# Layer 0 of a graph network: which message tiles are kept whole in fp32 for the segment sum

## The reference, cut to what matters

```python
src, dst = (edge_index[0], edge_index[1])
msg = jax.nn.relu(x[src] + edge_attr @ W_e + b_e)          # (21250, 512)
aggr = jax.ops.segment_sum(msg, dst, num_segments=x.shape[0])
h = (1.0 + eps) * x + aggr
h = jax.nn.silu(_bn(h @ W1 + b1, g1, beta1))
h = h @ W2 + b2
return jax.nn.silu(_bn(h, g2, beta2))
```

## Time and profile before

| | us |
|---|---|
| median of 3 runs | 855.38 |
| the three runs | 850.87 to 858.94 |
| the profiled execution, its own time | 855.74 |
| its span, first to last instruction | 853.9 |
| mean granted TensorE clock | 0.971 of full |

### The profile page before, as it was taken

One profiled execution on the slowest core, in us unless ns is written; L12 is line 12 of the kernel. 1 busy time (PEld: TensorE's weight loads), 2 busy tenths in 40 slices (PEclk: granted clock), 3 DMA queues, 4 the chain that ended last, 5 costly groups with the idle time before them and its releaser, 6 DMA issues.

```text
span 853.9 us, 11369 instructions
## 1 busy us (share of the span) xinstructions
PE 781.4 (92%) x3714; PEld 629.9 (74%) x3714; DVE 638.5 (75%) x1120; ACT 448.8 (53%) x805; POOL 359.6 (42%) x381
## 2 busy tenths in 40 slices
PE   7899998888879999798699999999999999999993
PEld 5665655565569999686477878788867898989893
DVE  7889998898679826387598999999984253535365
ACT  4888988888554403211377777787761211111122
POOL 6777777777300000023777777777700000000011
PEclk9999999999889999889799999999999999999996
DMA  8999888888500050014678888888820220200011
GB/s 231 327 322 307 264 264 246 256 251 252 202 2 1 1 197 1 1 50 146 204 249 289 261 258 259 259 264 261 245 79 1 74 75 1 74 1 1 1 50 71
DMA packets 49389, 134.38 MB, mean 157 GB/s; under 512 B 8265, under 2 KB 8521, under 8 KB 48944
## 3 DMA queue, kind: packets, MB, share of 16 engines
q0 software_dynamic: 26720, 87.58, 33.4%
q1 hardware_dynamic: 22116, 45.59, 16.3%
q10 hardware_dynamic: 492, 0.45, 0.2%
HBM read 128.47 MB, written 5.12 MB: 156 GB/s over the span
## 4 chain that ended last, share of the span: by engine, by line
PE 58%; DMA 12%; POOL 11%; DVE 10%; issue 6%; ACT 3%; SPq 0%; DVEq 0%; POOLq 0%; ACTq 0%
PE banks L512 37%; PE banks L539 10%; POOL raw L442 10%; DMA raw<-in_x,src_sb 7%; PE banks L569 4%; PE banks L570 3%; DMA raw<-table_dram,src_sb 3%; DVE msg_lo L1107 2%; DVE raw L1115 2%; DMA x_in<-in_x 2%; DVE stats L1245 1%; ACT banks L846 1%; PE banks L583 1%; PE banks L592 1%; DVE last L1405 1%
## 5 line engine op out<-in xcount | busy, mean ns | idle before, releaser
L442 POOL DMA_INDIRECT raw<-in_x,src_sb x167 | 168.0, 1006 | 52.3 <-issue 42.3
L442 POOL DMA_INDIRECT raw<-table_dram,src_sb x167 | 163.8, 981 | 61.1 <-issue 34.7
L464 POOL TENSOR_TENSOR moments<-moments,minus_half 128x1 f32<-128x1 f32 x32 | 20.3, 635 | 319.5 <-DVE moments L1251 319.5
L846 ACT ACTIVATE banks<-raw 128x512 f32<-128x512 f32 x166 | 99.1, 597 | 68.4 <-DMA raw<-table_dram,src_sb 35.9
L1115 DVE TENSOR_TENSOR raw<-banks,raw 128x512 f32<-128x512 f32 x168 | 114.3, 681 | 20.6 <-PE banks L539 15.9
L1107 DVE SCALAR_TENSOR_TENSOR msg_lo<-raw,msg_hi 128x512 fp32r<-128x512 f32 x168 | 113.9, 678 | 10.2 <-ACT msg_hi L890 9.6
L890 ACT ACTIVATE msg_hi<-raw 128x512 fp32r<-128x512 f32 x168 | 104.7, 623 | 31.0 <-DVE raw L1115 28.9
L569 PE MATMUL banks<-msg_hi,hot 128*128 128x512 f32 x293 | 116.6, 398 | 0.7 <-DVE agg L1130 0.4
L570 PE MATMUL banks<-msg_lo,hot 128*128 128x512 f32 x293 | 115.3, 393 | 0.0
L539 PE MATMUL banks<-We_hi,attr 97*128 97x512 f32 x167 | 87.5, 524 | 20.7 <-ACT banks L846 19.3
L1107 DVE SCALAR_TENSOR_TENSOR msg_lo<-banks,msg_hi 128x512 fp32r<-128x512 f32 x125 | 84.6, 677 | 1.8 <-ACT msg_hi L890 1.6
(11 more groups left out here) (170 smaller groups left out, 1725.2 us busy)
## 6 DMA issues: line engine op xcount, KB each, us to landing
attr_sb<-in_attr SPq DMA_DIRECT2D x84, 128.0 KB, 4.5
attr_sb<-in_attr SPq DMA_DIRECT2D x42, 256.0 KB, 4.0
Wg_raw<-in_Wg SPq DMA_DIRECT2D x3, 1536.0 KB, 6.4
raw<-in_x,src_sb POOLq DMA_INDIRECT x167, 4.9
raw<-table_dram,src_sb POOLq DMA_INDIRECT x167, 4.2
x_in<-in_x SPq DMA_DIRECT2D x5, 512.0 KB, 13.2
rows<-in_x SPq DMA_DIRECT2D x1, 2560.0 KB, 12.3
table_dram<-table_sb SPq DMA_DIRECT2D x9, 256.0 KB, 2.0
```

The source lines that it names most:

```text
L442: pool.indirect_dma_start(rows_of(L, t), None, tables[L], bass.IndirectOffsetOnAxis(ap=src_sb[:, t:t + 1], axis=0)).then_inc(gathered[t % ...
L464: nc.gpsimd.tensor_tensor(moments[:, slot * 4 + 2:slot * 4 + 3], moments[:, slot * 4 + 1:slot * 4 + 2], minus_half[:, 0:1], ALU.pow).then_ ...
L846: return nc.scalar.activation(to, of, ACT.Copy)
```

## The change

`whole` now holds for every odd tile of layer 0, which are all the placed ones: 83 tiles of 167. The 42 tiles 1, 5, ..., 165 are added to it. For these ACT writes `msg_whole`, DVE makes no low part, and PE makes one fp32 product in place of two fp32r passes. The counts of `lows` and the waits that depend on them follow. Layer 1 is as it was.

```diff
         def whole(L, t):

-            return L == 0 and t % 4 == 3
+            return L == 0 and odd(t)

         def lows(L, tiles):
```

## The result

The change makes the kernel slower: 867.72 us (median of 4 runs, 866.9 to 869.75) against 856.54 (850.87 to 858.94), a ratio of 1.0164 with a 95% interval of 1.0129 to 1.0199. The prediction was no measurable change, 856.6 us in a range of 851 to 861.5. The result lies outside it.

The account below looks back on a forecast made before the run. POOL's issue of gathers was taken to bound layer 0's edges. Profiled 855.74 + 0 in steady state + 1.25 for the tail = 857.0, less 0.36 to the median: 856.6 us, range 851 to 861.5.

Parts of the forecast that it names:

- POOL's issue of gathers bounds layer 0: Layer 0's edges: 167 unbroken gathers of 1006 ns with 0.3 us gaps set the pace, 5.22 us per four tiles.
- The gathers themselves get shorter: Second rival, layer 0: less DVE work shortens gathers, 10.2 us if all excess goes (846), a quarter 854; chance 0.05.
- The row meant to exclude the link: Layer 0: a gather at 109.19 beside two low parts took 0.94 us, cited against DVE's work lengthening gathers.
- The second argument against it: Layer 1: DVE makes every low part, yet gathers average 981 ns, cited against DVE's work lengthening gathers.
- The sentence on the Trainium skill's rule: DVE and GpSimd share SBUF ports; removed low parts, with one SBUF input, hold nothing and would give nothing back.
- DVE's 25 us turned into waiting: Layer 0 on DVE: 42 low parts gone, 25.2 us, become waiting off the path; value zero.
- PE's price: Layer 0 on PE: an fp32 product costs 0.41 us extra per tile, 17.2 us in all; zero in steady state.
- The cover: PE's spare time per four tiles against the gathers' 5.22 us shrinks from 0.93 to 0.52 us but holds.
- The third rival: Layer 0: PE takes POOL's place, the ring's slack runs out and gathers are held, 10.6 us, 867; chance 0.07.
- The tail: End of layer 0's edges, where PE is the bound: last edge pass 1.25 us later, ends 0 and 2.1.
- the fourth rival: End of layer 0: only PE's slow-clock stretch and the transfers move, 853 to 860 us; chance 0.07.
- The signs named ahead: Profile after: 84 low parts, 166 L567, last gather near 221, weight load 209, edge pass 233, L512 242.6 (wrong outside 238 to 248).

Follow-up runs that it names:

- the first trace: Profiled execution of the changed kernel in the main measurement, no further edit: 868.26 us.
- after_again: The changed kernel run once more, no edit: 868.0 us, ratio 1.0135 to the kernel before.
- dve_back: Changed kernel with DVE's 42 removed low parts made again, unread, and the earlier waits; PE keeps its 83 fp32 sums: 858.46 us, ratio 1.0036 to the kernel before.
- the second trace: Profile of the changed kernel run once more without edit (after_again): 868.0 us.
- bank_add_before: Kernel before, with DVE's add of an even tile written to its PSUM bank, so relu and low part read PSUM: 860.91 us, ratio 1.0066.
- after_control: Changed kernel, no edit, on a chip where the kernel before takes 963.83 us: 961.06 us, ratio 0.9958.

## Why the prediction was wrong, point by point

- That POOL's issue of gathers bounds layer 0 was right, and it carried the result: nearly all of the loss is POOL's own time (10.7 us of 12.5 in the first trace, 10.9 of 11.9 at the first MLP product in the second).
- The failed step is "The gathers themselves get shorter" and the zero that it left in the sum, that is, the assumption that 1006 ns would stay. The term measured +10.7 and +10.9 us in the two traces. The link between DVE's work and the gathers' length, which that rival considered, is real; only its sign was taken for granted, less work on DVE, shorter gathers. The opposite was never priced.
- The row meant to exclude the link was misread. "The gather at 109.19 ran beside two low parts", but it had started 0.14 us before the first of them. What counts is what DVE is in when a gather starts. The longer gathers stood in the trace, each with such an operation ahead of it; "nothing else in the trace explains the longer ones" was written without laying them beside DVE's. The second argument against it, layer 1's 981 ns though DVE makes every low part there, counts operations where their place counts: layer 1 has as many two-input operations as layer 0, with a third of the starts under them.
- The sentence on the Trainium skill's rule was right in that the removed low parts "hold nothing and would give nothing back". What was missed is that they kept a place free: without them, operations that do hold come to stand where gathers start (20 free starts gone; 21 to 24 more under one-hots).
- DVE's 25 us turned into waiting, as predicted: between 40 and 200 us it stands 28.2 us for PE's products, 23.3 more than before.
- PE's price held: the whole sum at 101.53 in the changed kernel is followed by its second edge pass at 102.62, 1.09 us later. Less one pass of 0.23 and against 0.46 for a split sum that is 0.40 us extra, where the prediction had 0.41. The cover held too: after 64 us POOL shows only the usual gaps of 0.3 us. The third rival named 867 us, which is close to the measured 867.72, but by a mechanism that after_again excludes: no ring wait, the same loss. dve_back prices PE's part at 2.5 us with DVE as before.
- The tail: from the last gather's start to the first MLP product it took 20.1 us before, 18.0 and 20.5 in the two traces after. Part of this is the fourth rival. The stretch at the lower clock (granted clock 0.76 and 0.56 of full in the two stretches of 5 us from 215 to 225 us before) came again in the second trace (0.76 and 0.56 from 225 to 235) but not in the first (1.00 from 200 to 250). With the slow stretch in both, the tail grew by 0.4 us where 1.25 was predicted, inside its ends of 0 and 2.1 and too small to be told. That the first trace lacks the slow stretch also hides its ring waits: its last gather starts 3.1 us later than the second's, its first MLP product only 0.5 us later.
- The signs named ahead: 84 even low parts and 166 entries of L567 came true. The last gather at 235.80 and 232.74 (predicted near 221), the weight load at 222.42 and 219.21 (209), the last edge pass at 244.15 and 243.62 (233) and the first L512 at 253.80 and 253.26 (wrong after 248) all failed, each by about the gathers' growth and, in the first trace, the ring waits.

## What to carry to other kernels

When an engine issues gathers back to back and bounds the stretch, look at every gather that is longer than the shortest, and at what DVE is in at its start; here operations that read two tensors from SBUF held it for their rest, and those with an input in PSUM didn't. Two loops of nearly fixed lengths (here gathers' starts 1.25 us apart and operations 0.60 apart) meet at places that repeat (the gathers of 1.6 us in bank_add_before come every 15.7 us), so taking work away from an engine that isn't the bound can cost more than it saves. Ask where such operations stand against the starts, not only how many there are. And a change that costs time where one engine sets the pace may gain where another does, as in after_control: price it for both.

## What the runs showed that was not expected

- A held gather lasts 0.945 us plus the rest of DVE's operation at its start less 0.12, within 0.015 in all 472 cases of layer 0 and all 124 of layer 1 in ten traces.
- A two-input operation that begins after the gather costs it nothing in layer 0 (none of 639 such gathers in the ten traces takes over 0.97 us; 109.19 in the earlier trace rows is one). Layer 1 has 54 exceptions in 1120, all with the operation beginning 0.09 to 0.14 us after the gather, which then lasts about 1.6 us (488.64 in bank_add_before). Why layer 0 has none of these is open.
- Useless work on DVE made the changed kernel 9.5 us faster (dve_back, 858.46 against 868.0 on the same chip).
- The same pair of kernels compares as 1.0164 on one chip and as 0.9958 on another on which the kernel before takes 964 us.
